# A four-stage transformer kernel on one Trainium2 core: the last feed-forward stage re-split over the engines, with b1 added by a rank-6 bf16 product and the rounded values transposed as fp16 bit patterns

## What is computed

```python
def activation_quant(x):                      # per token
    scale = 127.0 / clip(max(abs(x), axis=-1), EPS)
    return clip(round(x * scale), -128.0, 127.0) / scale
def weight_quant(w):
    scale = 1.0 / clip(mean(abs(w)), EPS)
    return clip(round(w * scale), -1.0, 1.0) / scale
def bitlinear(x, w, b):
    return einsum('bsd,fd->bsf', activation_quant(x), weight_quant(w)) + b

h = bitlinear(layernorm_without_affine(x), w1, b1)   # 256 -> 1024
h = gelu(h)
h = layernorm(h, gamma, beta)                        # over the 1024
x = x + bitlinear(h, w2, b2)                         # 1024 -> 256
```

## Time and profile before

| | us |
|---|---|
| median of 3 runs | 479.3 (478.52 to 481.51) |
| the profiled execution's own time | 479.36 |
| its span in the trace | 477.5 |
| busy: DVE, ACT, PE, POOL | 379.8, 308.2, 308.0, 150.2 |
| last stage, 404 to 478 us, busy: DVE, ACT, PE, POOL | 52.8, 42.0, 36.8, 38.2 |

### The profile page before, as it was taken

The page is one execution under the profiler, slowest core; times in us unless marked ns, Lnnn a source line. Parts: engine busy times, 40 slices in busy tenths (PEclk is TensorE's granted clock), DMA queues, the critical chain, the costliest instruction groups (busy, mean ns, idle before and its releaser), DMA issues.

```text
span 477.5 us, 7398 instructions
## 1 busy us (share of the span) xinstructions
PE 308.0 (65%) x2562; PEld 198.0 (41%) x2562; DVE 379.8 (80%) x647; ACT 308.2 (65%) x483; POOL 150.2 (31%) x252
## 2 busy tenths in 40 slices
PE   1987656447644378676748776777676767724545
PEld 1654445434213367554424444444444444402324
DVE  2438788994998979657578999998999999478975
ACT  2436244346711125558997999999999989566750
POOL 2600124330257923020121123121312132177760
PEclk9989876756956659887697999899989999855766
DMA  8700002111000000021399999799898979300001
GB/s 257 279 1 1 0 10 86 81 28 62 0 0 1 1 1 1 0 45 23 71 235 171 175 147 168 130 166 171 145 148 162 161 124 158 42 0 1 23 23 44
DMA packets 115637, 39.91 MB, mean 84 GB/s; under 512 B 110480, under 2 KB 114192, under 8 KB 114832
## 3 DMA queue, kind: packets, MB, share of 16 engines
q1 hardware_dynamic: 114592, 38.39, 40.8%
q0 software_dynamic: 144, 0.52, 0.4%
q10 hardware_dynamic: 864, 0.53, 0.4%
HBM read 11.11 MB, written 1.05 MB: 25 GB/s over the span
## 4 chain that ended last, share of the span: by engine, by line
DVE 25%; ACT 24%; PE 20%; issue 17%; POOL 9%; DMA 3%; POOLq 1%; SPq 0%; DVEq 0%; ACTq 0%
ACT rb L712 15%; POOL ra L496 3%; DVE nm L1156 3%; PE ps L1627 2%; DVE rb L1077 2%; PE ps L1565 2%; POOL small L501 2%; PE ps L1407 2%; ACT ra L762 2%; DMA stage<-rb 2%; PE ps L1536 2%; DMA cx<-ctx_in 2%; PE ps L1639 1%; POOL rb L452 1%; DVE rb L1066 1%
## 5 line engine op out<-in xcount | busy, mean ns | idle before, releaser
L1156 DVE TENSOR_REDUCE nm<-ps 128x1 f32<-128x1024 f32 x128 | 153.2, 1217 | 17.8 <-PE ps L1627 17.4
L712 ACT ACTIVATE rb<-ps,eb,sq 128x1024 int16<-128x1024 f32 x128 | 153.7, 1215 | 8.2 <-POOL eb L474 7.6
L1627 PE MATMUL ps<-ra,rb 128*128 128x512 bf16 x256 | 84.4, 417 | 41.5 <-ACT rb L712 40.7
L474 POOL TENSOR_SCALAR eb<-nm,sq 128x1 f32<-128x1 f32 x128 | 34.2, 267 | 148.0 <-DVE nm L1156 147.5
L1627 PEld LDWEIGHTS ps<-ra,rb 128*128 128x128 bf16 x256 | 16.2, 102 | 61.2 <-ACT rb L712 58.9
L1557 PE MATMUL ps<-idb,gs 128*128 128x128 bf16 x128 | 13.6, 270 | 40.8 <-DVE gs L1243 26.6
L452 POOL TENSOR_TENSOR rb<-rb 128x2048 f32<-128x2048 f32 x5 | 26.8, 5356 | 32.2 <-DVE rb L1066 29.1
L1652 PEld LDWEIGHTS ps<-ra,tern 128*128 128x128 f16 x624 | 25.3, 97 | 13.4 <-issue 1.0
L647 ACT ACTIVATE sB<-ps,small 128x1024 int16<-128x1024 f32 x8 | 8.9, 1113 | 33.0 <-DVE small L1099 33.0
L1557 PEld LDWEIGHTS ps<-idb,gs 128*128 128x128 bf16 x128 | 10.5, 122 | 46.9 <-DVE gs L1243 31.2
L1536 PE MATMUL ps<-xqT,tern 128*128 128x512 bf16 x64 | 20.1, 459 | 12.7 <-DVE rb L1066 11.6
(11 more groups left out here) (181 smaller groups left out, 710.8 us busy)
## 6 DMA issues: line engine op xcount, KB each, us to landing
stage<-w SPq DMA_DIRECT2D x2, 1024.0 KB, 4.8
rb<-ra SPq DMA_DIRECT2D x16, 128.0 KB, 2.9
rb<-wide_rows SPq DMA_DIRECT2D x1, 1536.0 KB, 7.3
xs<-x SPq DMA_DIRECT2D x4, 256.0 KB, 8.1
cx<-ctx_in SPq DMA_DIRECT2D x4, 256.0 KB, 8.3
stage<-w_gate SPq DMA_DIRECT2D x1, 1024.0 KB, 10.2
stage<-w_up SPq DMA_DIRECT2D x1, 1024.0 KB, 12.2
stage<-w_down SPq DMA_DIRECT2D x1, 1024.0 KB, 4.8
```

What stands on the lines that cost most here:

```text
L474: nc.gpsimd.tensor_scalar(eb[:, u % 3:u % 3 + 1], nm[:, u % 3:u % 3 + 1], sq[:, t, h:h + 1], LN255, ALU.mult, ALU.add).then_inc(s_bias, 1)
L712: A(esc[u % E_RING], bank(2 * (u % 3), 2), ACT.Exp, bias=eb[:, u % 3:u % 3 + 1], scale=sq[:, t, h:h + 1], accum_out=es[:, t % 2, h:h + 1]) ...
L1156: V.tensor_reduce(nm[:, u % 3:u % 3 + 1], bank(2 * (u % 3), 2), AX.X, ALU.max, negate=True).then_inc(s_max, 1)
L1627: ins = M(bank(2 * (u % 3) + hf), qz[t % 2][:, h // 2, h % 2, :], kT[:, h // 2, 512 * hf:512 * hf + 512], start=True, stop=True)
```

## The change

In the last stage the work is split anew:

- **b1 moves to PE.** The sum that Gelu needs is sd·(q·w) + b1 = sd·(q·w + b1/sd). b1 is split into three bf16 parts and 1/sd into three, and their six leading products are added to the PSUM sum as one matmul of 32 contraction rows and 512 columns per bank (`aT` times `bpart`). DVE's `f_bias` is gone, and `gelu(t)` reads PSUM with `scale=sd`. POOL splits b1 in 28 steps (`b1_part`, 128x256 each) behind the biases of units 24 to 51, and 1/sd in 6 small steps (`inverse_part`) behind those of units 120 to 125, with 6 more in the last stage for tiles 6 and 7. PE transposes these parts (`inverse_transposes`), and DVE copies them out (`inverse_rows`).
- **Normalising** is no longer an ACT pass. DVE does (h - mean)·gamma (`f_centre`) and then times rstd plus beta (in `f_scales`), both 128x1024 with two SBUF inputs; POOL's 128x1024 product with gamma is gone.
- **Rounding and transposing.** ACT adds 128 while rounding to int16, so that all values are positive; the 16 bits are transposed on PE as fp16 patterns without a conversion, ACT copies them out of PSUM as 512 int32 per row (`fT_out`), and `f_down` multiplies them by W2 in fp16. The 128 is taken out by a ninth matmul of 256 columns with the column sums of W2 (`corr2`), which `column_sums` (8 matmuls) and one DVE instruction prepare once, at the start of the attention loop.
- The lags of the calls become: ACT `gelu(t)`, `f_round(t-2)`, `fT_out(t-3)`, `f_squares(t)`; DVE `f_scales(t-1)`, `f_centre(t)`, `f_residual(t-4)`; POOL `f_minus_mean(t)`, `f_rstds(t)`, `f_factors(t-1)`. On POOL `ln(3, 3)` and `x3_b2(7)` now stand ahead of `f_minus_mean(0)`; on DVE the closing of query tile 7 stands ahead of the loop.

```diff
 @block.gpsimd
+            def b1_part(step, piece):
+                c = slice(D * piece, D * piece + D)
+                x, y = bwork[:, 0, :], bwork[:, 1, :]
+                if step == 0:
+                    pool.wait_ge(ld_wide, 16)
+                    pool.wait_ge(w_tern, 5)
+                    ins = nc.gpsimd.tensor_copy(bpart[:, c], rowv["b1"][:, c])
+                elif step in (1, 4):
+                    ins = nc.gpsimd.tensor_scalar(y, bpart[:, c], col[:, 6 + step // 4:7 + step // 4], 1.0, ALU.mult, ALU.mult)
+                elif step in (2, 5):
+                    ins = nc.gpsimd.tensor_tensor(x, rowv["b1"][:, c] if step == 2 else x, y, ALU.add)
+                else:
+                    ins = nc.gpsimd.tensor_copy(bpart[:, c], x)
...
+                if B_FIRST <= u < B_FIRST + B_STEPS * B_PIECES:
+                    b1_part((u - B_FIRST) % B_STEPS, (u - B_FIRST) // B_STEPS)
+                if A_FIRST <= u < A_FIRST + 6:
+                    inverse_part(u - A_FIRST, slice(0, T - 2))
...
+            ln(3, NP - 1)
+            x3_b2(T - 1)
             for t in range(T + 1):
                 if t < T:
                     f_minus_mean(t)
-                if t == 0:
-                    ln(3, NP - 1)
-                    x3_b2(T - 1)
+                    f_rstds(t)
+                if t == 1:
+                    for step in range(6):
+                        inverse_part(step, slice(T - 2, T))
                 if t >= 1:
-                    f_gammas(t - 1)
-                if t < T:
-                    f_rstds(t)
+                    f_factors(t - 1)
 @block.scalar
             def gelu(t):
-                act.wait_ge(f_h, t + 1)
-                A(hw[t], hw[t], ACT.Gelu, accum_out=fsum[:, t:t + 1]).then_inc(f_gelu, 1)
+                act.wait_ge(f_ps, t + 1)
+                act.wait_ge(f_sd, t // 2 + 1)
+                A(hw[t], bank(WIDE_BANK[t % 2], 2), ACT.Gelu, scale=sd[:, t:t + 1],
+                  accum_out=fsum[:, t:t + 1]).then_inc(f_gelu, 1)
...
+            def fT_out(t):
+                act.wait_ge(f_tr, t + 1)
+                if t >= 2:
+                    act.wait_ge(f_dn, t - 1)
+                A(fTi[:, t % 2, :], bank(t % 2).bitcast(I32), ACT.Copy).then_inc(f_tr_sb, 1)
 @block.vector
             attention(2)
+            dve.wait_ge(c2_ps, 1)
+            V.tensor_scalar(corr2[0:1, :], bank(7)[0:1, 0:D], -SHIFT / FP16_UNIT, None, ALU.mult).then_inc(c2_sb, 1)
             for u in range(FIRST, U + O_LAG):
                 attention(u)
...
+            def f_centre(t):
+                dve.wait_ge(f_mean, t + 1)
+                V.scalar_tensor_tensor(out=centred[t % 2], in0=hw[t], scalar=fneg[:, t:t + 1], in1=rowv["gamma"],
+                                       op0=ALU.add, op1=ALU.mult).then_inc(f_centred, 1)
             def f_scales(t):
...
+                link(V.scalar_tensor_tensor(out=hw[t], in0=centred[t % 2], scalar=frs[:, c], in1=rowv["beta"],
+                                            op0=ALU.mult, op1=ALU.add))
 @block.tensor
             def widen(t):
                 pe.wait_ge(xq_tr_sb, NP + t // 2 + 1)
+                pe.wait_ge(b_parts, B_PIECES)
+                g = 0 if t < 4 else 1 + (t - 4) // 2
+                pe.wait_ge(a_tr_sb, g + 1)
                 if t >= 2:
-                    pe.wait_ge(f_h, t - 1)
+                    pe.wait_ge(f_gelu, t - 1)
+                r = slice(32 * (t % 4), 32 * (t % 4) + 32)
                 for hf in range(2):
+                    b = bank(WIDE_BANK[t % 2] + hf)
+                    M(b, aT[r, g, :], bpart[r, 512 * hf:512 * hf + 512], start=True, stop=False)
...
             pe.wait_ge(q_four, NP)
             pe.wait_ge(wp_set, 1)
+            column_sums()
+            pe.wait_ge(c2_sb, 1)
```

More of the change, by code:

```diff
@@ L775, in _ @@
                     o_out(T - 1)
-                if t == 1:
-                    gelu(1)
+                if 2 <= t < T + 2:
+                    f_round(t - 2)
                 if t >= 3:
-                    f_round(t - 3)
-                if 1 <= t <= T:
-                    f_normalise(t - 1)
+                    fT_out(t - 3)
                 if t < T:
@@ L1678, in widen, with f_transposes, f_down @@
                 ins.then_inc(f_ps, 1)
+            def f_transposes(t):
+                pe.wait_ge(f_int, t + 1)
+                if t >= 2:
+                    pe.wait_ge(f_tr_sb, t - 1)
+                for c in range(FC):
+                    ins = TR(half_bank(t % 2)[:, P * c:P * c + P], fi16[:, t % 2, P * c:P * c + P], idh[:, :])
+                ins.then_inc(f_tr, 1)
+            def f_down(t):
+                b = bank(6 + t % 2)[:, 0:D]
+                w = tern[:, W2, :].bitcast(F16)
+                if t >= 2:
+                    pe.wait_ge(f_out, t - 1)
+                M(b, one16[0:1, :], corr2[0:1, :], start=True, stop=False)
+                pe.wait_ge(f_tr_sb, t + 1)
+                for c in range(FC):
+                    ins = M(b, fT16[:, t % 2, P * c:P * c + P], w[:, D * c:D * c + D], start=False, stop=(c == FC - 1))
+                ins.then_inc(f_dn, 1)
@@ L1680, in _, with column_sums @@
+            def column_sums():
+                pe.wait_ge(w_tern, 5)
+                pe.wait_ge(shift_set, 1)
+                w = tern[:, W2, :].bitcast(F16)
+                for c in range(FC):
+                    ins = M(bank(7)[0:1, 0:D], one16[:, 0:1], w[:, D * c:D * c + D], start=(c == 0), stop=(c == FC - 1))
+                ins.then_inc(c2_ps, 1)
             for t in range(T + 1):
@@ L1774 @@
     bv = a["L1_xattn_bkv"][D:]
+    first, second = np.zeros(32, f32), np.zeros(32, f32)
+    first[[1, 2, 4]] = -1.0
+    second[2] = -1.0
     row_of = {"bq": "L1_xattn_bq", "bp": "L1_xattn_bp", "b2": "L1_ffn_b2", "b1": "L1_ffn_b1",
@@ L1782 @@
         "cols": np.stack([twice(a["L0_xattn_theta_b"]), twice(a["L0_xattn_phi_b"]), twice(a["L0_xattn_g_b"]),
-                          a["L0_xattn_out_b"], bv[:P], bv[P:]], axis=1),
+                          a["L0_xattn_out_b"], bv[:P], bv[P:], np.tile(first, 4), np.tile(second, 4)], axis=1),
         "ident": np.eye(P, dtype=f32),
```

171 lines of the change are left out of this document (102 added, 69 removed).

## The result

| | before | after |
|---|---|---|
| median of 20 runs each, us | 477.2 (471.82 to 482.61) | 474.35 (470.63 to 479.81) |
| ratio | 1 | 0.994, 95% interval 0.991 to 0.997 |
| profiled execution, us | 479.36 | 471.81 |
| its span, mean granted TensorE clock | 477.5, 0.821 | 470.0, 0.829 |

The account below looks back on a forecast made before the run. The last stage was taken as bound by a chain of waits between POOL and ACT, 5.94 us a turn. Last stage -9.9, attention loop's entry +3.3 and b1 steps +0.3 gave -6.3: 479.36 to 473.1 us, range 469.5 to 477.5.

Parts of the forecast that it names:

- Period: Eight turns of the last stage: DVE sets the period, 4.72 us a turn instead of 5.94.
- Entry of the attention loop: Start of the attention loop: PE's column sums and DVE's correction add a wait on the critical path, +3.3 us.
- b1 on POOL: Attention loop: POOL's 28 b1 steps are mostly hidden behind the biases, +0.3 us (0 to 1).
- Tail: End of the last stage, through the last `f_residual`: 5.7 us, between 3.8 at PE's 2.4 GHz and 6.7 at 1.2.
- Entry of the last stage: From the attention loop into the last stage: `o_scale` starts near 412.4 us, +0.85; first `f_scales` ends at 427.0.
- the wait behind two `f_bias` gone: Entry of the last stage: `o_scale` no longer waits behind two `f_bias`, which had lasted until 411.56 us.
- four rank 6 products: Entry of the last stage: two widens have 4 x 512 columns more at the upper clock, 0.9 us.
- the late fourth copy: Entry of the last stage: `widen(0)` waits for a fourth PSUM copy on DVE, 0.75 us later.
- The entry's delay: Rival, attention loop: the 3.3 us vanishes in PE's later wait for a transposed unit, 469.8 us; chance 0.12.
- DVE waits for POOL: Rival, last stage: wide DVE steps wait for POOL's small steps, 0.8 us a turn, 478.9 us; chance 0.12.
- PE at 1.2 GHz: Rival, last stage: PE stays slow, the tail is 6.7 us and `f_down` late, about 475 us; chance 0.08.
- POOL's steps hold the biases: Rival, attention loop: b1 steps over 0.9 us delay DVE and ACT; from 1.3 us a step, 484.3 us; chance 0.06.

Follow-up runs that it names:

- e1_sums_early: Changed kernel with the column sums of W2 and their correction moved ahead of the first feed-forward block's mixing; 471.12 us, 0.981 of before.
- e5_b1_four_steps: Changed kernel with POOL doing only the first of seven steps per b1 piece, so b1's other parts are wrong; 474.90 us, 0.991 of before.
- e7: Changed kernel with DVE copying the transposed 1/sd factors before the tokens, and without the product that adds b1; 469.38 us, one run.
- e8: Changed kernel with early column sums, both widens behind the last output projection, and the 1/sd factors copied before the tokens; 467.45 us, 0.980 of before.
- e3: Changed kernel with the column sums moved early and both widens issued behind the last output projection; 467.61 us, 0.979 of before.
- e9: Changed kernel with 14 useless transposes on PE filling the wait ahead of the first widen; 469.75 us, one run.
- e6: Changed kernel with DVE copying the transposed 1/sd factors before the three token copies; 472.87 us, 0.989 of before.

## Why the prediction was right in direction and twice too large

474.35 lies in the range of 469.5 to 477.5, but 1.25 us above the forecast of 473.1, which was made against a slower median for before (479.3; over 20 runs it is 477.2). That the time came so near the forecast is luck of that baseline: counted as differences, -6.3 was forecast and -2.85 came. The forecast gave 0.68 to a gain of over 1% and 0.27 to what came, a change within 1%. Of the forecast's steps:

**Period: right.** 4.72 forecast, 4.62 measured, DVE full from tile 3 on, and 32.13 us for seven turns instead of 41.60. Collisions of DVE's wide steps with POOL's small ones were priced at 0.6 us over all turns. DVE's waits for POOL's late results are 0.33 and 0.51 ahead of the third and the fourth `f_scales` and 0.11 ahead of each of the last four, 1.3 in all. DVE's steps made up for it by standing closer: 4.51 a turn without the gap, where 4.72 was forecast. From `o_scale` to the end of the last `f_scales` the forecast was 47.4 us and 46.45 came.

**Entry of the attention loop: right.** +3.3 forecast; +3.15 measured, and e1_sums_early took it away whole. The terms too: sums 1.92 (1.87), correction 0.41 (0.41).

**b1 on POOL: right in kind.** +0.3 forecast, +0.5 measured by e5_b1_four_steps.

**Tail: 0.6 too short.** 5.7 forecast from the last reciprocal, 6.32 measured (461.55 to 467.87). The two levels were put at 3.8 and 6.7. The runs give 4.9 (e7, e8, PE's last pieces at the upper clock) and 7.2 (e3, e9, clock 0.50); after lay between.

**Entry of the last stage: the step that failed.** "So `o_scale` starts near 412.4: +0.85." It started 4.23 later than before relative to the first copy. Four parts, each from a run:

| | forecast | measured |
|---|---|---|
| the wait behind two `f_bias` gone | about -0.8 | -0.75 (4.03 to e7's 3.28) |
| four rank 6 products | +0.9 | +1.58 (e7 to e6) |
| the late fourth copy | +0.75 | +0.78 (e6's 4.86 to e5's 5.64) |
| PE at the lower clock | 0 | +2.6 (e5's 5.64 to after's 8.26) |

The sentence "two widens have 4 x 512 columns more at the upper clock" holds both errors: the columns were counted and the cost of a product of another shape was not, and the clock of the earlier trace rows was carried over to a place ahead of which the change puts a wait. The prediction had the clock as a rival for the tail and for `f_down`; it didn't ask what the clock would be at the entry, where the row of before showed the upper level. The measured parts are 4.2 us, 3.4 more than forecast. With the tail's 0.6, less the 0.95 that the stretch from `o_scale` to the last `f_scales` came in under, that is, to rounding, the 3.07 between -9.9 and -6.83. The lower clock costs more than its line in the table: that stretch came in under although 1.2 us of it are the clock. From `o_scale` to the start of the first `f_scales` 11.7 was forecast and 11.4 came, and 10.2 where PE had its upper clock (e5).

**The rivals.** The entry's delay was not absorbed: the loop is 0.64 us longer, and 0.5 of that is b1. *DVE waits for POOL*: it had 0.8 us a turn; 0.11 came, and not as that rival had it. The Trainium skill, page "SBUF — State Buffer", section "Who interferes with whom", lets either side of the port pair block the other. These traces agree for POOL (0.19 becomes 1.22, 0.61 becomes 1.55). For DVE they do not show it. Its 0.11 is the wait for L562's result. Its wide step L1301 begins 0.1 us into POOL's L567, which has some 0.15 us to go (444.77 against 444.67), and takes 1.285 there, against 1.278 for the first one in e3_both, where POOL ran nothing. *PE at 1.2 GHz* did come, at another place than the rival had it: 2.6 us up to `o_scale` and 1.2 behind it. Against e5_b1_four_steps it is 2.94 over the whole stage, the upper end of the rival's +1.0 to +2.9. *POOL's steps hold the biases*: no, the longest takes 0.72.

## What to carry to other kernels

An edit that frees the bound engine in a stage is worth what is left when its own preparations are paid for: here 9.5 us came out of the turns, and 3.15 + 4.2 went into two places where new work for TensorE was put ahead of a chain that something waited for. Such work had slack elsewhere, and moving it made the difference between 0.6% and 2%. Before a row's duration on TensorE is used behind a new wait, work the sum at both clock levels, and take a matmul of another operand height as dearer than its columns. And where the chain of waits names a tiny step with a large duration, look in the timeline at which wide step of another engine it began under.
